# Order of scatters, source gathers and base gathers on POOL in the last edge stage of a four-layer graph network

## The chip, the cores and the metric

The kernel runs on one core of a Trainium2 chip, and its time is the device time of one execution in microseconds (us). A lower number is better. The engines are PE (TensorE), DVE (VectorE), ACT (ScalarE), POOL (GpSimd) and SP (SyncE); each works through its own list of instructions in order, and they wait for one another by semaphores.

## What is computed

The reference is a graph network of four residual layers on 10000 nodes of 512 features and 5000 edges, sorted by the node they go to. Every layer normalises the node rows, and passes messages along the edges. Only the last layer is touched here, by the change as by the prediction:

```
x = inputs @ W_gcn                                  # 512 -> 128
msg = x[src] * edge_attr[:, None]
h = segment_sum(msg, dst, num_segments=N) + b_gcn
return h @ W_fc.T + b_fc                            # 128 -> 512
...
h = jnp.maximum(_layernorm(x, axis=-1), 0.0)
x = x + L3(h, edge_index, edge_weight, W_gcn, b_gcn, W_fc, b_fc)
```

## The kernel before, in words

Stages follow one another: edges and nodes of layer 0, messages, sums and nodes of layer 1, edges and nodes of layer 2, and last `layer3_edges`. The stage before it has already written to `out`, for every node, the row that holds without any edge. `layer3_edges` has to add to those rows of `out` what the edges bring.

The 5000 edges lie in 40 tiles of 128 partitions (`ET`), and four tiles make a group, so that there are 10 groups (`EG`), numbered 0 to 9. The stage's lists of instructions, one for each engine:

- **POOL** issues every transfer of the loop, as indirect DMAs of 128 rows by 512 floats. `rows(g)` (line 2447) gathers the four tiles of source rows of group g from `x3` into `X`, which has room for all 40 tiles. `base(g)` (line 2457) gathers the rows of `out` to which the group will be added into half g % 2 of `Z`; it first waits until the group two earlier has been stored from that half. `finished(g)` (line 2466) waits, tile by tile, for DVE's sum in `Z` and scatters it to `out`. Ahead of the loop stand `rows(0)` to `rows(2)`, `base(0)`, `base(1)` and a gather of 40 further rows into `Zc` (line 2475), and behind it the scatter of `Zc` (line 2485).
- **DVE** has, in `body(g)`, first the statistics of the four tiles of group g + 2 (line 2543), each waiting for its gather; between them the low parts of the transposed rows of group g + 1 (`turned`, line 2562); then the low part of the sums of group g (line 2588), and only then the four sums `Z = z + Z` of group g (`finish`, line 2576), which POOL's scatters wait for.
- **PE** transposes group g + 1 (line 2626), multiplies it by `W_gcn` (`product`, lines 137 to 139 into `m_ps`), and then multiplies the sums of group g by `W_fc` (`out`, lines 137 to 139 into `z_ps`), which `finish` adds. A transpose waits for DVE to have read the buffer that it writes to.
- **ACT** copies between them, and scales the rows of group g + 2.

`body` runs for g = 0 to 7 in full, for 8 without statistics, and for 9 without statistics and transposes. The order of POOL's three pieces in a turn of the loop is written out by hand: `rows(g + 3)`, `finished(g)`, `base(g + 2)`. The order in DVE's `body` is:

```
for j in range(GROUP):
    if norm:
        dve.wait_ge(x_loaded[j], g * 16 + 48)
        stats(g + 2, b, j)
    if turn:
        turned(g + 1, j)
...
finish(g, b, 0)
```

Of the kernel before, what the change touches and what calls it, by code (L numbers as in the profile page):

```python
# [2380 lines left out]
def layer3_edges(nc, core, a, keep, x3, match, out):  # L2381
# [16 lines left out]
    with ExitStack() as st:  # L2398
# [34 lines left out]
        with nc.Block() as block:  # L2433
            @block.sync
            def _(sp):
                sp.dma_start(Wraw[:, :, :], a["L3_gnn_W_gcn"].rearrange("(k p) n -> p k n", p=P)).then_inc(w_loaded, 16)
                sp.dma_start(Wf[:, :], a["WfT"]).then_inc(w_loaded, 16)

            @block.gpsimd
            def _(pool):  # L2440
                def rows(g):

                    for t in range(g * GROUP, g * GROUP + GROUP):
                        if t >= GROUP:
                            pool.wait_ge(x_loaded[t % GROUP], 16 * (t // GROUP))
                            pool.sem_inc(go, 1)
                        pool.indirect_dma_start(X[:, t, :], None, x3[:, :], bass.IndirectOffsetOnAxis(keep["src"][:, t:t + 1], 0),  # L2447
                                                bounds_check=ROWS_N - 1, oob_is_err=False).then_inc(x_loaded[t % GROUP], 16)

                def base(g):  # L2450

                    if g >= 2:
                        pool.wait_ge(stored[g % 2], 64 * (g // 2))
                        pool.sem_inc(go, 1)
                    for j in range(GROUP):
                        t = g * GROUP + j
                        pool.indirect_dma_start(Z[:, g % 2, j, :], None, out[:, :], bass.IndirectOffsetOnAxis(keep["goes"][:, t:t + 1], 0),  # L2457
                                                bounds_check=NODES - 1, oob_is_err=False).then_inc(base_loaded[g % 2], 16)

                def finished(g):  # L2460

                    for j in range(GROUP):
                        t = g * GROUP + j
                        pool.wait_ge(z_out, t + 1 + 2)
                        pool.sem_inc(go, 1)
                        pool.indirect_dma_start(out[:, :], bass.IndirectOffsetOnAxis(keep["goes"][:, t:t + 1], 0), Z[:, g % 2, j, :], None,  # L2466
                                                bounds_check=NODES - 1, oob_is_err=False).then_inc(stored[g % 2], 16)

                for g in range(3):
                    rows(g)  # L2470
                pool.wait_ge(init, 3)
                pool.sem_inc(go, 1)
                base(0)
                base(1)
                pool.indirect_dma_start(Zc[:, :], None, out[:, :], bass.IndirectOffsetOnAxis(keep["head_goes"][:, 0:1], 0),
                                        bounds_check=NODES - 1, oob_is_err=False).then_inc(last_loaded, 16)
                for g in range(EG):
                    if g + 3 < EG:
                        rows(g + 3)
                    finished(g)  # L2480
                    if g + 2 < EG:
                        base(g + 2)
                pool.wait_ge(z_out, ET + 1 + 2)
                pool.sem_inc(go, 1)
                pool.indirect_dma_start(out[:, :], bass.IndirectOffsetOnAxis(keep["head_goes"][:, 0:1], 0), Zc[:, :], None,
                                        bounds_check=NODES - 1, oob_is_err=False).then_inc(last_stored, 16)
                for b in range(2):
                    pool.wait_ge(stored[b], 64 * (EG // 2))
                pool.wait_ge(last_stored, 16)
# [312 lines left out]
```

## Time and profile before

| | |
|---|---|
| median of 3 runs | 2776.52 us |
| lowest, highest | 2774.21, 2776.92 us |
| the profiled execution: its own time | 2777.23 us |
| the profiled execution: its span | 2775.5 us |
| mean granted TensorE clock, share of full | 0.93 |
| busy share of the span: PE, DVE, ACT, POOL | 86%, 57%, 39%, 30% |

A profile shows one execution. The span goes from its first instruction to its last, and its own time is a little longer. Busy shares are means over stages that have different limits. A view of a stretch in time tells which instructions ran there, how long each one took, how long its engine had been idle before it, and what ended that idle time ("<-"). For an indirect DMA on POOL the time shown is that of issuing it; the data land later.

### The profile page before, as it was taken

What the parts mean: (1) busy time and instruction counts of PE and PEld (TensorE: products, weight loads), DVE (VectorE), ACT (ScalarE), POOL (GpSimd) and SP (SyncE); (2) the same over time, 40 slices, a digit from 0 to 9 for tenths busy, and PEclk for the clock granted to TensorE, in tenths of its full rate; (3) what the DMA queues carried; (4) which work ended last, traced back from release to release, by engine and by line L of the source; (5) the groups of instructions that cost most, each with busy time, mean ns of one, the idle gap of its engine ahead of it and who ended that gap; (6) DMA issues with size and microseconds to landing.
All of it is one profiled execution on the core that took longest, in us unless ns stands there. A gap on an engine that the chain in (4) does not pass through costs nothing. (4 is left out here: it accounts for less than half of the span.)

```text
span 2775.5 us, 39392 instructions
## 1 busy us (share of the span) xinstructions
PE 2393.4 (86%) x13443; PEld 2047.9 (74%) x13443; DVE 1568.3 (57%) x3060; ACT 1078.7 (39%) x1858; POOL 825.5 (30%) x684
## 2 busy tenths in 40 slices
PE   7889999999999899999999799955777348999465
PEld 7878888989989789999999688854232237777364
DVE  6733232332323566666666633385999657787554
ACT  2234333333433334333333356633665443333332
POOL 1001010101000211111111144345997345665566
PEclk9999999999999899999999889978888689999788
DMA  6101010101002333323333234324565584766444
GB/s 213 47 9 58 19 57 19 57 19 47 19 15 82 103 112 113 106 105 121 125 133 112 79 110 121 91 79 168 190 218 189 174 278 168 263 250 228 145 153 133
DMA packets 118895, 327.93 MB, mean 118 GB/s; under 512 B 25965, under 2 KB 39405, under 8 KB 100763
## 3 DMA queue, kind: packets, MB, share of 16 engines
q1 hardware_dynamic: 75186, 229.79, 23.0%
q0 software_dynamic: 42336, 97.19, 11.9%
q8 instruction: 39, 0.64, 0.1%
q14 instruction: 38, 0.30, 0.0%
q10 hardware_dynamic: 1296, 0.01, 0.0%
HBM read 245.35 MB, written 128.49 MB: 135 GB/s over the span
## 5 line engine op out<-in xcount | busy, mean ns | idle before, releaser
L137 PE MATMUL b_y_ps<-W23h,b_Rh 128*128 128x320 f32 x800 | 249.2, 311 | 0.0
L138 PE MATMUL b_y_ps<-W23l,b_Rh 128*128 128x320 f32 x800 | 246.0, 308 | 0.0
L139 PE MATMUL b_y_ps<-W23h,b_Rl 128*128 128x320 f32 x800 | 246.0, 308 | 0.0
L1055 POOL DMA_INDIRECT c_G<-T,c_idx x80 | 83.5, 1043 | 452.1 <-DVE c_U L1152 429.8
L137 PE MATMUL b_hid_ps<-b_hTh,W1h 128*128 128x512 f32 x500 | 201.1, 402 | 7.9 <-ACT b_Rh L668 7.9
L137 PE MATMUL c_u_ps<-W1h,c_hTh 128*128 128x320 f32 x640 | 201.2, 314 | 1.0 <-DVE c_U L1152 1.0
L139 PE MATMUL b_hid_ps<-b_hTh,W1l 128*128 128x512 f32 x500 | 199.9, 400 | 0.0
L138 PE MATMUL b_hid_ps<-b_hTl,W1h 128*128 128x512 f32 x500 | 199.9, 400 | 0.0
L138 PE MATMUL c_u_ps<-W1l,c_hTh 128*128 128x320 f32 x640 | 197.7, 309 | 0.0
L139 PE MATMUL c_u_ps<-W1h,c_hTl 128*128 128x320 f32 x640 | 197.7, 309 | 0.0
L766 DVE TENSOR_TENSOR b_Rl<-b_R,b_Rh 128x512 fp32r<-128x512 f32 x100 | 69.2, 692 | 226.9 <-ACT b_Rh L668 226.9
L608 POOL DMA_INDIRECT b_X<-in_x,b_idx x32 | 32.3, 1009 | 490.9 <-PE b_tp_ps L869 482.4
L1966 PE MATMUL n_z_ps<-n_G,n_D 128*128 128x512 f32 x160 | 98.9, 705 | 76.0 <-ACT n_D L1846 32.4
L137 PE MATMUL c_o_ps<-W1h,c_zh 128*128 128x512 f32 x400 | 163.2, 408 | 0.0
L138 PE MATMUL c_o_ps<-W1l,c_zh 128*128 128x512 f32 x400 | 158.0, 395 | 0.0
L139 PE MATMUL c_o_ps<-W1h,c_zl 128*128 128x512 f32 x400 | 157.8, 395 | 0.0
L1092 ACT ACTIVATE c_R<-c_tp_ps,c_b 128x512 f32<-128x512 f32 x100 | 69.0, 690 | 224.7 <-PE c_tp_ps L1235 224.7
L791 DVE TENSOR_TENSOR b_Yl<-b_y_ps,b_Yh 128x320 fp32r<-128x320 f32 x80 | 39.3, 491 | 202.8 <-ACT b_Yh L680 202.8
L138 PEld LDWEIGHTS b_y_ps<-W23l,b_Rh 128*128 128x128 f32 x800 | 150.1, 188 | 0.5
L137 PEld LDWEIGHTS b_y_ps<-W23h,b_Rh 128*128 128x128 f32 x800 | 150.0, 188 | 0.5
L139 PEld LDWEIGHTS b_y_ps<-W23h,b_Rl 128*128 128x128 f32 x800 | 149.9, 187 | 0.0
L667 ACT ACTIVATE b_R<-b_hid_ps,b 128x512 f32<-128x512 f32 x100 | 68.9, 689 | 184.1 <-PE b_hid_ps L139 173.5
(417 smaller groups left out, 6941.4 us busy)
## 6 DMA issues: line engine op xcount, KB each, us to landing
b_X<-in_x SPq DMA_DIRECT2D x21, 1024.0 KB, 5.2
x<-n_O SPq DMA_DIRECT2D x20, 1032.0 KB, 4.9
g_X<-x SPq DMA_DIRECT2D x20, 1032.0 KB, 6.9
x<-c_XB SPq DMA_DIRECT2D x20, 1028.0 KB, 4.5
n_X<-x SPq DMA_DIRECT2D x20, 1028.0 KB, 7.3
x<-g_O SPq DMA_DIRECT2D x20, 1024.0 KB, 3.8
c_XB<-in_x SPq DMA_DIRECT2D x19, 1024.0 KB, 5.4
out<-g_B SPq DMA_DIRECT2D x19, 1024.0 KB, 4.8
```

What stands on the lines that cost most here:

```text
L137: pe.matmul(out, ah, bh, start=first, stop=False)
L138: pe.matmul(out, ah, bl, start=False, stop=False)
L139: return pe.matmul(out, al, bh, start=False, stop=last)
L608: pool.indirect_dma_start(X[:, i // GROUP, i % GROUP, :], None, a["x"][:, :], bass.IndirectOffsetOnAxis(idx[:, i:i + 1], 0), bounds_check= ...
L667: act.activation(R[:, :], hid[:, m % 2, :], ACT.Relu, bias=l0["b1"][:, m:m + 1]).then_inc(relu_ready, 1)
L766: dve.tensor_tensor(Rl[:, m, :], R[:, :], Rh[:, m, :].bitcast(F32), ALU.subtract).then_inc(hid_lo, 1)
L791: dve.tensor_tensor(Yl[:, t % 2, w], y[:, h, 0:HALF], Yh[:, t % 2, w].bitcast(F32), ALU.subtract).then_inc(y_out[h], 1)
L1055: pool.indirect_dma_start(G[:, i // GROUP, i % GROUP, :], None, T0[:, :], bass.IndirectOffsetOnAxis(idx[:, i:i + 1], 0), bounds_check=ROWS ...
L1092: act.activation(R[:, k % 2, :], tp[:, k % 2, :], ACT.Relu, bias=b3[:, c:c + 1]).then_inc(z_hi, 1)
L1966: pe.matmul(z[:, i, :], D[:, g % 2, j, :], G[:, g % RG, j, :], start=True, stop=False)
```

## The change

In each turn of POOL's loop the scatters of group g are issued first, then the source gathers of group g + 3, then the base gathers of group g + 2. Nothing else is changed.

```
                 for g in range(EG):
+                    finished(g)
                     if g + 3 < EG:
                         rows(g + 3)
-                    finished(g)
                     if g + 2 < EG:
                         base(g + 2)
```

POOL's list at the start of the loop, before; `h_X<-x3,src` are the source gathers, `out_0<-h_Z,goes` the scatters, `h_Z<-out_0,goes` the base gathers:

```order
L2447 DMA h_X<-x3,src 128x512 x12
L2457 DMA h_Z<-out_0,goes 128x512 x8
L2475 DMA h_Zc<-out_0,headgoes 40x512
L2447 DMA h_X<-x3,src 128x512 x4
L2466 DMA out_0<-h_Z,goes 10000x512 x4
L2457 DMA h_Z<-out_0,goes 128x512 x4
L2447 DMA h_X<-x3,src 128x512 x4
L2466 DMA out_0<-h_Z,goes 10000x512 x4
```

And in the changed kernel:

```order
L2447 DMA h_X<-x3,src 128x512 x12
L2457 DMA h_Z<-out_0,goes 128x512 x8
L2475 DMA h_Zc<-out_0,headgoes 40x512
L2466 DMA out_0<-h_Z,goes 10000x512 x4
L2447 DMA h_X<-x3,src 128x512 x4
L2457 DMA h_Z<-out_0,goes 128x512 x4
L2466 DMA out_0<-h_Z,goes 10000x512 x4
L2447 DMA h_X<-x3,src 128x512 x4
```

The four source gathers of each turn went from the place before the four scatters to the place between them and the four base gathers.

DVE's list in one turn is the same in both kernels; `h_raw` is written by the statistics, `h_hTl` by `turned`, and `h_Z` by the sums that the scatters wait for:

```order
L2543 BN_STATS h_raw<-h_X 128x6
L2562 TENSOR_TENSOR h_hTl<-h_tp_ps,h_hTh 128x512
L2543 ISA
L2543 BN_STATS h_raw<-h_X 128x6
L2561 REGISTER_ALU
L2562 TENSOR_TENSOR h_hTl<-h_tp_ps,h_hTh 128x512
L2547 ISA
L2550 BN_AGGR h_mv<-h_raw 128x2 x4
L2588 TENSOR_TENSOR h_Sl<-h_s_ps,h_Sh 128x512
L2575 ISA
L2576 TENSOR_TENSOR h_Z<-h_z_ps,h_Z 128x512 x2
```

Nothing moved there: the rows are the first and the last two of the four pairs of statistics and `turned`, and what follows them up to the first sums.

## Rows read from the trace of the kernel before

**Rows 1.** Busy time by stretch: us, PE, PEld, DVE, ACT, POOL, granted clock, DMA share, GB/s.

```profile
2680.00:2698.00 18.00, 11.72 (x60) 10.23 (x60) 9.23 (x21) 6.55 (x11) 12.10 (x13) 0.78 0.48 149
```

**Rows 2.** Timeline of POOL in one turn: start, us, operation [idle before <-releaser].

```profile
2675.26 1.00 POOL L2447 DMA_INDIRECT h_X<-x,src  x1 [0.30 <-issue]
...
2680.47 1.04 POOL L2466 DMA_INDIRECT out<-h_Z,goes  x1 [0.30 <-issue]
...
2684.41 0.98 POOL L2466 DMA_INDIRECT out<-h_Z,goes  x1 [0.30 <-issue]
2687.94 1.04 POOL L2457 DMA_INDIRECT h_Z<-out,goes  x1 [2.54 <-DMA out<-h_Z,goes]
...
2693.21 1.00 POOL L2447 DMA_INDIRECT h_X<-x,src  x1 [0.31 <-issue]
...
2698.42 1.03 POOL L2466 DMA_INDIRECT out<-h_Z,goes  x1 [0.30 <-issue]
```

**Rows 3.** Who waited for whom, 2626 to 2747: us in total, times, longest.

```profile
POOL h_Z L2457 <- DMA out<-h_Z,goes: 17.8, 7, 2.7
```

**Rows 4.** Timeline of DVE and PE in the same turn.

```profile
2678.82 0.69 DVE L2543 BATCH_NORM_STATS2 h_raw<-h_X 128x6 f32 x1 [5.77 <-DMA h_X<-x,src]
...
2683.52 0.63 PE L139 MATMUL h_m_ps<-h_hTh,h_Wl 128*128 128x512 f32 x1
2683.95 0.63 PE L137 MATMUL h_m_ps<-h_hTh,h_Wh 128*128 128x512 f32 x1
...
2687.14 0.40 PE L137 MATMUL h_z_ps<-h_Wfh,h_Sh 128*128 128x512 f32 x1
...
2689.24 1.32 DVE L2576 TENSOR_TENSOR h_Z<-h_z_ps,h_Z 128x512 f32<-128x512 f32 x2
```

**Rows 5.** Timeline of POOL: first source gather of four more turns.

```profile
2639.42 1.00 POOL L2447 DMA_INDIRECT h_X<-x,src  x1 [0.30 <-issue]
...
2657.34 1.00 POOL L2447 DMA_INDIRECT h_X<-x,src  x1 [0.30 <-issue]
...
2711.09 0.99 POOL L2447 DMA_INDIRECT h_X<-x,src  x1 [0.30 <-issue]
...
2729.01 1.00 POOL L2447 DMA_INDIRECT h_X<-x,src  x1 [0.30 <-issue]
```

**Rows 6.** Timeline of DVE: first two sums of a group, in the six turns.

```profile
2652.42 1.29 DVE L2576 TENSOR_TENSOR h_Z<-h_z_ps,h_Z 128x512 f32<-128x512 f32 x2 [2.76 <-PE h_z_ps L139]
...
2669.91 1.29 DVE L2576 TENSOR_TENSOR h_Z<-h_z_ps,h_Z 128x512 f32<-128x512 f32 x2 [2.29 <-PE h_z_ps L139]
...
2687.43 1.29 DVE L2576 TENSOR_TENSOR h_Z<-h_z_ps,h_Z 128x512 f32<-128x512 f32 x2 [2.07 <-PE h_z_ps L139]
...
2705.02 1.29 DVE L2576 TENSOR_TENSOR h_Z<-h_z_ps,h_Z 128x512 f32<-128x512 f32 x2 [1.55 <-PE h_z_ps L139]
...
2722.49 1.29 DVE L2576 TENSOR_TENSOR h_Z<-h_z_ps,h_Z 128x512 f32<-128x512 f32 x2 [1.25 <-PE h_z_ps L139]
...
2741.56 1.29 DVE L2576 TENSOR_TENSOR h_Z<-h_z_ps,h_Z 128x512 f32<-128x512 f32 x2 [2.34 <-PE h_z_ps L139]
```

**Rows 7.** Timeline at the first group: its first two sums, its first scatter.

```profile
2624.86 1.29 DVE L2576 TENSOR_TENSOR h_Z<-h_z_ps,h_Z 128x512 f32<-128x512 f32 x2 [0.87 <-PE h_z_ps L139]
...
2626.50 1.03 POOL L2466 DMA_INDIRECT out<-h_Z,goes  x1 [5.93 <-DVE h_Z L2576]
```

**Rows 8.** By line: one sum; time from a source gather's issue to its landing.

```profile
L2576 DVE TENSOR_TENSOR h_Z<-h_z_ps,h_Z x40: 680/691/694, 2624.9 to 2764.0; 128x512 f32<-128x512 f32 x40
...
DMA to landing us min/median/max: 3.5/3.7/5.2
```

**Rows 9.** Timeline of the end: groups 7 to 9.

```profile
2746.88 1.03 POOL L2466 DMA_INDIRECT out<-h_Z,goes  x1 [0.30 <-issue]
...
2757.39 0.40 PE L139 MATMUL h_z_ps<-h_Wfh,h_Sl 128*128 128x512 f32 x1
...
2761.29 1.29 DVE L2576 TENSOR_TENSOR h_Z<-h_z_ps,h_Z 128x512 f32<-128x512 f32 x2 [4.52 <-DMA h_Z<-out,goes]
```

More of the change, by code:

```diff
@@ L2477, in _ @@
                 for g in range(EG):
+                    finished(g)
                     if g + 3 < EG:
                         rows(g + 3)
-                    finished(g)
                     if g + 2 < EG:
```

## The prediction

> **What bounds the kernel now.** The change touches only the last stage, so I read the busy time by stretch first, then POOL's timeline of one turn, then who waited for whom, and last DVE's and PE's timelines, to see what the instruction behind each wait had itself waited for. In 18 us of the steady loop no compute engine is busy more than 12 us [rows 1]. POOL's list is what sets the pace: from one group's first source gather to the next group's it takes 17.95 us (2675.26 to 2693.21), and almost all of its gaps are the 0.30 us between two issues [rows 2]. One gap is longer: the first base gather waits 2.54 us until the scatters issued before it have landed. It comes in every turn, 17.8 us over 7 of them [rows 3]. Three pieces of four issues and this wait make the turn. One piece takes 5.2 us: source gathers 2675.26 to 2680.47, 5.21; scatters 3.94 to the start of the fourth, and 0.98 and 0.30 for it and its gap, 5.22; base gathers 2687.94 to 2693.21, 5.27, the first of them 0.05 longer after the wait. Of a turn without that wait 15.7 us would be left.
>
> The same rows tell that DVE waits for POOL: its first statistics instruction sat idle 5.77 us until the first source gather had landed, 3.56 us after its issue [rows 2, 4]. The sums that the scatters need come later in DVE's list than these statistics. Now the scatters don't feel that: the first sums of that turn begin at 2687.43, and the scatter that wants them is issued at 2698.42, 10.3 us after the first is done at 2688.12 (0.69 us for one) [rows 2, 6, 8].
>
> **The change part by part.** No instruction is added or taken away; 28 source gathers (seven turns of four) move behind 28 scatters.
>
> The wait for the scatters' landing: the source gathers now stand between the scatters and the base gathers. They take 5.21 us, and the wait was 2.54 us, so the base gathers find the scatters landed. Gain: up to 2.5 us in each of seven turns. Turn 7 has no source gathers, and its wait stays.
>
> The new order closes a loop. Source gathers of group g + 3 used to be issued before the scatters of group g, which need nothing from them. They are now issued after them, and the next thing but the base gathers is the scatters of group g + 1. These need the sums of group g + 1, which in DVE's list stand behind the statistics of group g + 3. Each turn is then, from scatter to scatter:
>
> - first sum done to first scatter issued: POOL is idle and waits, as it did for the first group. The sum ends at 2624.86 + 0.69 = 2625.55, and the scatter starts at 2626.50 [rows 7, 8]: 0.95 us.
> - four scatters, until the first source gather: 5.22 us.
> - first source gather issued to the first sum begun. Six turns show it while DVE waits for the gather, as it will: 13.00, 12.57, 12.17, 11.81, 11.40 and 12.55 us (each start in rows 6 less the gather's in [rows 2, 5]), on average 12.25.
> - the first sum: 0.69 us [rows 8].
>
> Together 19.11 us. The fourth sum is done 2.4 us after the first (2689.24 + 1.32 against 2688.12 [rows 4]) and the fourth scatter starts 3.9 us after the first, so only the first sum counts. POOL's own work of 15.7 us fits into this, and POOL will stand idle for about 3.4 us ahead of each first scatter; queued behind that wait are the source gathers on which DVE waits in turn. DVE, PE and ACT get nothing new to do, and their work is inside the 12.25 us.
>
> Sum: from the first scatter of group 0 to that of group 7 it took 2746.88 - 2626.50 = 120.38 us [rows 7, 9]. The first group's scatter stays where it is, because its sums wait for nothing that moves; POOL waited 5.93 us for them already [rows 7]. Seven turns of 19.11 make 133.77, which is 13.39 us more. A part of that comes from the last of the seven, which held no source gathers before, and now does.
>
> The end: from the first scatter of group 7 the base gathers of group 9 follow as before, and 14.41 us after that scatter the sums of group 9 begin (2761.29), having waited 4.52 us for those gathers [rows 9]. This wait was cover for PE, and it shrinks: PE's product for that sum was ready at 2757.79, 15.54 us after the first sum of group 7 (2741.56 + 0.69) [rows 6, 9]. With the scatter now 0.95 us behind that sum, the gathers are in at 15.36. So PE is late by 0.2 us, and the tail grows by that. In all +13.6 us against the profiled execution's 2777.23 us: 2790.8. The median of the runs is 0.7 us below that execution, so I forecast **2790.1 us**, 0.49% slower.
>
> What no row shows is the landing of a gather issued straight behind four scatters; in the trace source gathers follow base gathers. The nearest rows give 3.5 at least and 5.2 us at most, with a median of 3.7 [rows 8]. I take the 3.56 us that is in the 12.25, because the queue carried the same bytes at the same pace before; with 5.2 us in each turn the sum would grow by 11.5 us, and a gain from it of more than 0.4 us in all is excluded by the minimum.
>
> The Trainium skill (DMA: Bandwidth & Descriptors, Anatomy of one DMA — SWDGE (gpsimd) path) gives 2.0 us plus the bytes at 436 GB/s for one transfer, an estimate of 2.6 us for these 256 KB; by that the turn would be 18.15 us and the time 2783.4. The trace has 3.56 us for this very transfer, so I keep 2790.1.
>
> **The rivals.** (a) Faster. The loop doesn't close, and POOL's issuing stays the bound: the turn shrinks to 15.7 us, seven take 109.9, and the time is 10.5 us lower, 2766.0. That holds if the first sum is done within 9.5 us of the first source gather's issue (two pieces of POOL's work, 10.4, less 0.95). For it speaks that the wait of 2.5 us is plainly on POOL's path [rows 2, 3]; against it, that the shortest of six turns needed 11.40 + 0.69 = 12.09. The Trainium skill (Perfetto Trace Analysis, Optimization Strategy) says to find the gaps on the engine that limits a stretch and make what ends them start or finish sooner, and by that rule this rival is the outcome. The gap is there as the rule wants it, but closing it puts another wait on the same engine. 5%.
>
> (b) No change. The new wait costs what the old one did: 17.9 us a turn from the first group on, seven times, make 125.3 us, 4.9 us more and 2781.4. For that, 11.0 us from gather to sum are needed, less than any of the six showed. 4%.
>
> (c) Slower still. PE's gap between groups grows with the turn. Its granted clock is 0.78 over this stretch [rows 1]: after the gap its matmuls start 0.43 us apart (2683.52, 2683.95), which is the lower level of 1.2 GHz. Later in the same turn it is back on the upper one: the 13 starts after 2683.52 take 3.62 us to 2687.14, and at 0.43 us each they would take 5.6 [rows 4]. If the clock stayed low through product and output, the 12.17 us of this turn would thus be 14.2. That is a turn of 21.0 us, and the time is 2803.5. Against it: none of the six turns came near 14.2. Late landings (5.2 us) end near the same time, 2801.6. 8% together.
>
> **How the numbers follow.** The forecast, a loop through DVE, has the remaining 83%. Its own bounds: all turns like the shortest (11.40) give 7.4 us more through the loop, 2784.1; all like the longest (13.00) give 18.6 more, 2795.3. The unpriced landing can add to that, so the range goes from 2784 to 2797; it leaves out (a), and most of (c). Measurement can tell about 0.2%, 5.5 us, from no change: faster 0.05, same 0.04, slower 0.91.
>
> **What would show it.** Right: first scatters about 19.1 us apart from 2626.5 on; the line of waits from base gathers to scatters down to one of 2.5 us, in turn 7; in its place a wait of scatters for DVE's sums, some 3.4 us in each turn; DVE's statistics still waiting for the source gathers, longer than 5.8 us. Wrong: scatters 15.7 us apart with no idle time before them would mean (a); a turn of 21 us with PE at 0.43 us a matmul up to the sums, or landings above 3.7 us, would mean (c).

## The result, and the profile after

The changed kernel takes 2786.99 us (median of 6 runs, 2785.44 to 2788.76), the kernel before 2775.36 us (6 runs, 2772.15 to 2776.92). The ratio is 1.0046 with a 95% interval of 1.0035 to 1.0058: slower by 11.6 us, where 13.6 were forecast, and inside the range of 2784 to 2797.

The profiled execution of the changed kernel took 2787.22 us. First, POOL's timeline: the first scatter of each of the groups 0 to 7.

```profile
2623.75 1.04 POOL L2466 DMA_INDIRECT out<-h_Z,goes  x1 [11.11 <-DVE h_Z L2576]
...
2642.36 1.02 POOL L2466 DMA_INDIRECT out<-h_Z,goes  x1 [3.17 <-DVE h_Z L2576]
...
2661.82 1.02 POOL L2466 DMA_INDIRECT out<-h_Z,goes  x1 [4.07 <-DVE h_Z L2576]
...
2680.15 1.02 POOL L2466 DMA_INDIRECT out<-h_Z,goes  x1 [2.94 <-DVE h_Z L2576]
...
2699.43 1.02 POOL L2466 DMA_INDIRECT out<-h_Z,goes  x1 [3.88 <-DVE h_Z L2576]
...
2717.74 1.02 POOL L2466 DMA_INDIRECT out<-h_Z,goes  x1 [2.94 <-DVE h_Z L2576]
...
2737.32 1.02 POOL L2466 DMA_INDIRECT out<-h_Z,goes  x1 [4.20 <-DVE h_Z L2576]
...
2757.04 1.02 POOL L2466 DMA_INDIRECT out<-h_Z,goes  x1 [4.32 <-DVE h_Z L2576]
```

The starts lie 18.61, 19.46, 18.33, 19.28, 18.31, 19.58 and 19.72 us apart, 133.29 us in all, where the kernel before took 120.38 [rows 7, 9]. In groups 1 to 7 each first scatter now stands behind an idle time of 2.9 to 4.3 us that a sum of DVE ends. Before, these scatters had only the 0.30 us between issues [rows 2]. Group 0 is apart: POOL waits 11.11 us instead of 5.93 [rows 7] there, because four source gathers no longer fill the first 5.2 us of that wait.

The rest of the turn from 2661.82 to 2680.15, on POOL and then on DVE:

```profile
2665.74 0.99 POOL L2466 DMA_INDIRECT out<-h_Z,goes  x1 [0.30 <-issue]
2667.03 1.05 POOL L2447 DMA_INDIRECT h_X<-x,src  x1 [0.30 <-issue]
2668.39 1.01 POOL L2447 DMA_INDIRECT h_X<-x,src  x1 [0.31 <-DMA out<-h_Z,goes]
...
2672.31 0.99 POOL L2457 DMA_INDIRECT h_Z<-out,goes  x1 [0.31 <-issue]
```

```profile
2670.64 0.69 DVE L2543 BATCH_NORM_STATS2 h_raw<-h_X 128x6 f32 x1 [7.27 <-DMA h_X<-x,src]
...
2678.55 1.29 DVE L2576 TENSOR_TENSOR h_Z<-h_z_ps,h_Z 128x512 f32<-128x512 f32 x2 [1.31 <-PE h_z_ps L139]
```

The base gathers follow the source gathers after 0.31 us; the 2.54 us of [rows 2] are gone from this place. DVE's first statistics sat idle 7.27 us (5.77 in [rows 4]), until the gather issued at 2667.03 had landed, 3.61 us later. The sums begin 11.52 us after that gather. Over the seven turns this is 11.77, 12.65, 11.52, 12.47, 11.51, 12.46 and 12.91 us, on average 12.18.

Who waited for whom, from 2626 to 2760 (total, times, longest), and then, from the lines of the gathers, what base gathers of the whole stage waited for, and how long source gathers took to land:

```profile
DVE h_raw L2543 <- DMA h_X<-x,src: 50.6, 15, 7.6
...
POOL out L2466 <- DVE h_Z L2576: 26.4, 10, 4.3
```

```profile
DMA out<-h_Z,goes: 2.5, 1
```

```profile
DMA to landing us min/median/max: 3.4/3.6/5.4
```

The wait of [rows 3], 17.8 us over 7 times, has shrunk to a single one of 2.5 us, in turn 7. In its place stand 26.4 us in which POOL waits for sums. Source gathers land about as fast behind scatters as they did behind base gathers (3.5/3.7/5.2 in [rows 8]).

The last turns, on POOL and on DVE:

```profile
2764.40 1.05 POOL L2457 DMA_INDIRECT h_Z<-out,goes  x1 [2.45 <-DMA out<-h_Z,goes]
...
2778.73 0.99 POOL L2466 DMA_INDIRECT out<-h_Z,goes  x1 [0.30 <-issue]
2780.02 0.96 POOL L2485 DMA_INDIRECT out<-h_Zc,headgoes  x1 [0.30 <-issue]
```

```profile
2755.44 1.29 DVE L2576 TENSOR_TENSOR h_Z<-h_z_ps,h_Z 128x512 f32<-128x512 f32 x2 [2.71 <-PE h_z_ps L139]
...
2772.07 1.29 DVE L2576 TENSOR_TENSOR h_Z<-h_z_ps,h_Z 128x512 f32<-128x512 f32 x2 [1.48 <-DMA h_Z<-out,goes]
```

From the first scatter of group 7 to the end of the span (2785.4) it is 28.36 us, and it was 28.62 before (2775.5 less 2746.88). The sums of group 9 begin 15.03 us after that scatter instead of 14.41, and the end doesn't feel it: from the base gathers on POOL issues one DMA after the other with 0.30 us between them, to the last. From the first scatter of group 7 to that of group 9 it is 17.84 us in both kernels. The difference of 0.26 us lies behind that, and no run here explains it.

The spans of the two profiled executions differ by 9.9 us (2785.4 and 2775.5): 12.91 through the loop, -0.26 in the tail, and -2.75 up to the first scatter (2623.75 and 2626.50), because this one reached the stage earlier. Its first source gather was issued at 2583.6 and not at 2586.3, though nothing ahead of the stage differs. From that gather to the first scatter both took 40.2 us.

### The profile page after: what moved, and what is told of

It reads as the page before. It is cut to its first block and busy times, and to the rows that moved or that the text cites. A ratio compares the mean times of both kernels' runs of the same rounds, so it can differ in the third digit from the quotient of the medians.

```text
span 2785.4 us, 39392 instructions
## 1 busy us (share of the span) xinstructions
PE 2394.3 (86%) x13443; PEld 2052.5 (74%) x13443; DVE 1568.4 (56%) x3060; ACT 1077.8 (39%) x1858; POOL 825.2 (30%) x684
## 3 DMA queue, kind: packets, MB, share of 16 engines
q0 software_dynamic: 42336, 97.19, 11.8%
```

## The experiments

The kernel before and the changed one differ in two things at once. Read round the loop, the list before is scatters of g, base gathers of g + 2, source gathers of g + 4. The changed one has the source gathers in front of the base gathers, and they are those of g + 3. The first two experiments do one of these each. Their edits, and that of the last experiment, are shown against the kernel before; those of the other two against the changed kernel.

**The swap alone.**

```
+                rows(3)
                 for g in range(EG):
-                    if g + 3 < EG:
-                        rows(g + 3)
                     finished(g)
+                    if g + 4 < EG:
+                        rows(g + 4)
                     if g + 2 < EG:
                         base(g + 2)
```

> Source gathers between scatters and base gathers, as in the changed kernel, but one group earlier: rows(3) ahead of the loop, then finished(g), rows(g+4), base(g+2). Theory (the loss comes from the lost lead of the source gathers, which closes a loop through DVE's statistics): the loop stays open, the gathers cover the scatters' landing, and POOL's issuing is the bound: first scatters 15.7 us apart in the first six turns and 12.7 in the seventh, 106.9 us from group 0 to group 7 against 120.4 before, so about 13 us below the kernel before, 2762. Rival (source gathers straight behind scatters are what costs, by late landing or by the queue): turns as in the changed kernel, 18.3 to 19.7 us, 2787, or at best no gain over the kernel before.

Measured: 2763.11 us, ratio to the kernel before 0.9947 (0.9934 to 0.9961). POOL's timeline of one turn, and the first base gather of turn 6, in which no source gathers are left:

```profile
2657.22 1.03 POOL L2466 DMA_INDIRECT out<-h_Z,goes  x1 [0.30 <-issue]
...
2661.15 0.99 POOL L2466 DMA_INDIRECT out<-h_Z,goes  x1 [0.30 <-issue]
2662.45 1.04 POOL L2447 DMA_INDIRECT h_X<-x,src  x1 [0.30 <-issue]
...
2667.72 1.00 POOL L2457 DMA_INDIRECT h_Z<-out,goes  x1 [0.30 <-issue]
...
2672.93 1.04 POOL L2466 DMA_INDIRECT out<-h_Z,goes  x1 [0.30 <-issue]
```

```profile
2727.41 1.05 POOL L2457 DMA_INDIRECT h_Z<-out,goes  x1 [2.50 <-DMA out<-h_Z,goes]
```

The turn is 15.71 us, and POOL has no gap in it but the 0.30 us between issues. Where no source gathers cover it, the wait for the scatters is back with its 2.50 us. So the place behind the scatters costs POOL's turn nothing here, and the swap by itself is worth 2.2 us a turn.

**The lead alone.**

```
                 for g in range(EG):
-                    if g + 3 < EG:
-                        rows(g + 3)
                     finished(g)
                     if g + 2 < EG:
                         base(g + 2)
+                    if g + 3 < EG:
+                        rows(g + 3)
```

> The order of pieces of the kernel before (scatters, base gathers, source gathers, read round the loop), but the source gathers one group later: finished(g), base(g+2), rows(g+3). Theory: the loop closes, now with the landing wait and the base gathers inside it as well: 0.95 + 5.22 + 2.5 + 5.27 + 12.25 + 0.69 = 26.9 us a turn, seven turns 188 us against 120.4 before, about 68 us above the kernel before, 2843. Rival (the place straight behind the scatters is what costs): turns of 17.9 us as before, 2776.

Measured: 2839.58 us, ratio 1.0224 (1.0209 to 1.0240). One turn on POOL:

```profile
2676.30 1.02 POOL L2466 DMA_INDIRECT out<-h_Z,goes  x1 [8.89 <-DVE h_Z L2576]
...
2683.76 1.05 POOL L2457 DMA_INDIRECT h_Z<-out,goes  x1 [2.54 <-DMA out<-h_Z,goes]
...
2689.04 1.00 POOL L2447 DMA_INDIRECT h_X<-x,src  x1 [0.30 <-issue]
...
2703.10 1.02 POOL L2466 DMA_INDIRECT out<-h_Z,goes  x1 [9.16 <-DVE h_Z L2576]
```

The seven turns take 185.7 us (2623.96 to 2809.69), 26.5 each where 26.9 were expected. Against the changed kernel the source gathers are issued later by the wait and four base gathers, 7.8 us, and the turn is longer by 7.5 (26.5 less 19.0). A source gather that is late by a microsecond now makes the turn about a microsecond longer. A lost group of lead thus costs 8.6 us a turn in the old order (17.9 to 26.5) and 3.3 us in the new one (15.7 to 19.0); the swap gives back a part of it, and the lead accounts for the loss.

**The loop opened at its other end.** The changed kernel's list on POOL stays, and DVE's order is changed: the first two sums of group g now stand ahead of the statistics of group g + 2.

```
                     for j in range(GROUP):
-                        if norm:
-                            dve.wait_ge(x_loaded[j], g * 16 + 48)
-                            stats(g + 2, b, j)
                         if turn:
                             turned(g + 1, j)
...
                     finish(g, b, 0)
                     finish(g, b, 1)
+                    if norm:
+                        for j in range(GROUP):
+                            dve.wait_ge(x_loaded[j], g * 16 + 48)
+                            stats(g + 2, b, j)
+                        mean(g + 2, b)
+                        scale(g + 2, b)
                     if turn:
                         weigh(g + 1)
```

On ACT `messages(g + 1)` goes ahead of `root` and `norm_rows`; the two lists were only changed together. As a control the same was done with POOL's list of the kernel before.

> POOL's list of the changed kernel, unchanged, with the same lead of three groups; DVE's list in a turn reordered: turned, low part of the sums, the first two sums of group g, and only then the statistics of group g+2, weigh and the last two sums; ACT copies the messages ahead of scaling the next rows. Theory (the loop closes because the sums stand behind the statistics in DVE's list): the first two scatters no longer wait for the gather, the last two wait until about 9.9 us after the first gather's issue instead of 14, so POOL's issuing is nearly the bound: turns of 15.7 to 17 us instead of 18.3 to 19.7, 2764 to 2773. Rival (the lead itself, or the place behind the scatters, sets the turn whatever DVE's order): turns of 18.3 to 19.7, 2787.

> The same DVE and ACT order with POOL's list of the kernel before: control. Theory: POOL's issuing with the landing wait is the bound there, so the turns stay at 17.9 us and the time at 2776, within 3 us. Rival (the new order of DVE and ACT is shorter in itself, wherever the gathers stand): turns below 17.5 us and a time below 2773.

Measured: with the changed kernel's list 2778.31 us, ratio to the kernel before 1.0013 (1.0004 to 1.0022); with the old list 2779.17 us, ratio 1.0013 (1.0004 to 1.0023). Who waited for whom in the first of them, 2626 to 2747, and its POOL around one turn:

```profile
DVE h_hTl L2560 <- ACT h_hTh L2506: 36.1, 27, 3.3
...
PE h_tp_ps L2623 <- ACT h_H L88: 9.4, 7, 1.5
...
POOL out L2466 <- DVE h_Z L2574: 13.3, 7, 3.1
```

```profile
2678.06 1.03 POOL L2466 DMA_INDIRECT out<-h_Z,goes  x1 [0.30 <-issue]
...
2682.01 0.98 POOL L2466 DMA_INDIRECT out<-h_Z,goes  x1 [1.62 <-DVE h_Z L2574]
...
2695.09 1.02 POOL L2466 DMA_INDIRECT out<-h_Z,goes  x1 [0.30 <-issue]
```

Waits of DVE for source gathers, 50.6 us in the changed kernel, don't occur in this list at all. In groups 1 to 7 the first scatter waits for nothing, and the turn settles at 17.0 us (after 18.6 and 17.5 for the first two). With the lead and POOL's order unchanged, the new order on DVE and ACT takes 8.7 us off the changed kernel (2786.99 to 2778.31), so DVE's list is part of the loop, as the theory has it. Taken as pairs, POOL's new order costs 11.6 us with the old order on DVE and ACT, and nothing that can be measured with the new one (2778.31 against the control's 2779.17).

The time expected (2764 to 2773) was missed by 5 us. I had left out that the scaling of the next rows on ACT, which used to lie beside PE's products, now stands between the statistics and PE's transposes. One round of that chain, from the statistics of one group to those of the next, on DVE, ACT, PE and DVE:

```profile
2675.97 2.46 DVE L2541 BATCH_NORM_STATS2 h_raw<-h_X 128x6 f32 x4
...
2680.03 2.93 ACT L88 ACTIVATE h_H<-h_X,h_shift,h_rstd 128x512 f32 x4 [0.63 <-DVE h_shift L2555]
...
2683.09 1.11 PE L2623 MATMUL h_tp_ps<-ident,h_H 128*128 128x128 f32 x4 [1.33 <-ACT h_H L88]
...
2691.86 1.29 DVE L2574 TENSOR_TENSOR h_Z<-h_z_ps,h_Z 128x512 f32<-128x512 f32 x2 [1.65 <-PE h_z_ps L139]
...
2693.07 2.46 DVE L2541 BATCH_NORM_STATS2 h_raw<-h_X 128x6 f32 x4
```

It takes 17.1 us, and in the chain that ended last from 2676 to 2693 no instruction of POOL and no transfer occurs: this round is the new bound. The last turns became longer too, 15.4 and 6.4 us instead of 12.6 and 5.2, together 4.0 us; the cause of that is open. The control has turns of 17.9 us from the second on, as expected, so the new order is not shorter in itself there; its first turn is 21.9 instead of 18.1 us, which fits the 4 us by which its time lies above the kernel before, where I had allowed 3.

**The clock.** The changed kernel with matmuls in PE's gap, for which PE's loop is also written out; the writing out was not run by itself:

```
                             turn(g + 1, 1 - b, j)
+                        if fill and j == 1:
+                            for _ in range(28):
+                                pe.matmul(m[:, :], Wfh[:, 0:P], Wfh[:, :], start=True, stop=True)
```

> The changed kernel, with 28 further matmuls of 128x512 on PE in each of the groups 1 to 7, where PE waits for DVE (their result is overwritten), so that PE is not idle there; PE's loop is written out. It is to tell how much of a turn is the clock coming back after PE's gap. Theory: with the clock on its upper level the first sum is ready 11.2 us or less after the first source gather instead of 12.1 on average, turns even out at 17.6 to 18.3 us instead of 18.3 to 19.7, and the time falls by 4 to 9 us against the changed kernel, to 2778 to 2783; it does not come below the kernel before by more than 2 us, since the loop is still closed. Rival (the clock's return is beside the path, and landings make the difference between turns): turns keep 18.3 to 19.7 us, 2787.

Measured: 2781.08 us, ratio to the kernel before 1.0018 (1.0009 to 1.0027), 5.9 us below the changed kernel. Busy time over two turns, of the changed kernel and then of this one (us, PE, PEld, DVE, ACT, POOL, granted clock, DMA share, GB/s):

```profile
2642.40:2680.20 37.80, 23.17 (x121) 20.06 (x120) 18.59 (x40) 12.91 (x23) 24.08 (x25) 0.77 0.45 143
```

```profile
2641.50:2677.50 36.00, 33.43 (x178) 26.80 (x177) 19.04 (x40) 13.07 (x23) 24.04 (x24) 1.00 0.48 151
```

And one turn of this kernel, from its first source gather to the next group's first scatter:

```profile
2664.72 1.04 POOL L2447 DMA_INDIRECT h_X<-x,src  x1 [0.31 <-issue]
...
2677.50 1.02 POOL L2466 DMA_INDIRECT out<-h_Z,goes  x1 [2.61 <-DVE h_Z L2576]
```

```profile
2675.90 1.29 DVE L2576 TENSOR_TENSOR h_Z<-h_z_ps,h_Z 128x512 f32<-128x512 f32 x2 [0.88 <-PE h_z_ps L139]
```

With PE kept busy the granted clock is 1.00 over both turns, the upper level, and the sums begin 11.18 us after the gather, 11.0 to 11.2 in each of the seven turns. All seven turns last 17.9 to 18.2 us. The two views below are of the changed kernel again, from the first source gather to the first sum in a short turn and in the long one after it:

```profile
2667.03:2678.55 11.52, 6.57 (x29) 5.86 (x30) 6.24 (x15) 3.14 (x6) 8.04 (x8) 0.70 0.60 176
2685.36:2697.83 12.47, 7.65 (x29) 6.58 (x30) 6.25 (x16) 4.01 (x8) 8.06 (x8) 0.59 0.57 166
```

The granted clock is 0.70 or 0.71 in the three stretches of 11.5 to 11.8 us, and 0.59 or 0.60 in the four of 12.5 to 12.9. In the short turn PE's matmuls of 128x512 start 0.23 us apart, the upper level, from the third of `product` on, at 2675.27; in the long one they start 0.41 to 0.43 us apart, the lower level, up to the eighth, at 2695.67. So the unevenness of the changed kernel, 18.3 to 19.7, comes from where in PE's work the clock returns. The return costs about 1 us a turn on average (19.0 against 18.0), and it is on the path because the loop runs through PE. By their times, the reordered lists and the held clock can't be told apart (1.0013 and 1.0018, with intervals that overlap); what differs is the waits, and the turns, 17.0 against 18.0 us.

**One more group of lead.**

```
+                rows(3)
+                rows(4)
                 for g in range(EG):
-                    if g + 3 < EG:
-                        rows(g + 3)
                     finished(g)
+                    if g + 5 < EG:
+                        rows(g + 5)
                     if g + 2 < EG:
                         base(g + 2)
```

> As the swap alone, with one more group of lead: rows(3) and rows(4) ahead of the loop, where POOL waits 5.9 us for the first sums, then finished(g), rows(g+5), base(g+2). Theory (POOL's issuing is the bound once the loop is open): five turns of 15.7 us and two of 12.7, 103.9 us from group 0 to group 7, 16.5 us less than before, 2760. Rival (PE, DVE and ACT become the bound at less than 15.7 us of work, or the first scatter comes later by the added 5.2 us): no better than the swap alone, 2762 or more.

Measured: 2760.18 us, ratio to the kernel before 0.9943 (0.9929 to 0.9956). Its first scatter, the first base gather of turn 5, and DVE's longest wait:

```profile
2626.04 1.03 POOL L2466 DMA_INDIRECT out<-h_Z,goes  x1 [0.74 <-DVE h_Z L2578]
...
2712.03 1.04 POOL L2457 DMA_INDIRECT h_Z<-out,goes  x1 [2.52 <-DMA out<-h_Z,goes]
```

```profile
DVE h_Z L2578 <- DMA h_Z<-out,goes: 30.5, 7, 6.2
```

The wait before the first scatter has shrunk from 5.93 us [rows 7] to 0.74, five turns take 15.7 us, and turn 5 with its wait of 2.52 us takes 12.7. DVE now waits for base gathers, that is, for POOL. The time is 15 us below the kernel before and 27 below the changed one. The swap alone lies within its interval, so the times don't tell the two versions apart; in the traces the way from the first scatter of group 0 to that of group 7 is 103.95 us here (103.9 expected) and 106.87 there.

## Why the prediction was right

The mechanism and the size came out as forecast; one small term, the tail, did not.

- **The wait that goes.** As forecast: the base gathers find the scatters landed, and the wait remains in turn 7 only.
- **The loop.** Forecast as 19.11 us a turn; measured 19.04 on average. Of its terms, 0.95 was 0.91 (2757.04 less 2755.44 + 0.69, the first sum of group 7), 5.22 was 5.21 (2661.82 to 2667.03), and 12.25 was 12.18. The swap alone, the lead alone and the reordered lists on DVE and ACT show that both ends are needed: the late gather, and the sums behind the statistics. That the averages agree to 0.1 us is in part luck: the six rows behind the 12.25 spread from 11.40 to 13.00, the seven turns after from 11.51 to 12.91, and both hold the clock's return, about 1 us, which the forecast took over with the rows and priced only in rival (c).
- **The unpriced landing.** The 3.56 us that I took were right; it is 3.61 in the turn shown, and the median is 3.6. The Trainium skill's fit (DMA: Bandwidth & Descriptors, Anatomy of one DMA — SWDGE (gpsimd) path) would have given an estimate of 2.6 us and 2783.4 in all, below every run; the measurement decides.
- **The first group.** Forecast to stay; 40.2 us after the first source gather in both.
- **The tail.** This step failed, by half a microsecond: I had the tail grow by 0.2 us because PE's product would be late. It didn't grow. The sums of group 9 still waited for their base gathers, 1.48 us, not for PE, and they are not on the path: POOL's issuing is, with the same 17.84 us from group 7 to group 9. That the whole tail came out 0.26 us shorter lies behind that stretch, and its cause is open.
- **The size.** 13.6 us forecast; 12.65 by the profiles (loop and tail), 11.6 by the medians, whose interval reaches from 9.7 to 16.1 us (0.35% to 0.58% of 2775.4).
- **Rival (a)**, POOL's issuing as the bound at 15.7 us, is what happens as soon as the lead is kept. There the Trainium skill's rule on gaps that I set beside it (Perfetto Trace Analysis, Optimization Strategy) holds: the gap of 2.5 us is closed, and the turn falls from 17.9 to 15.7 us. The changed kernel closes the same gap and loses, because the same edit puts another wait on the same engine. **Rival (b)** would need sums 11.0 us after the gather. Even with the clock held they took 11.1 and the time stayed 0.18% above the kernel before, so (b) nearly describes that experiment, not the change. **Rival (c)** didn't occur: no turn came to 21 us.

## What to carry to other kernels

When a piece of a hand-written list is moved past a wait, count in groups how far ahead of its use it is issued afterwards: here one line's move cost a whole group of lead, and with that a transfer's latency and a chain through three engines came to stand inside every turn. The gain and the loss of such an edit can be taken apart, and here the gain was had by moving the piece, adding one group to its index and issuing that group ahead of the loop. Then price the chain from the issue to the wait it feeds by rows of the kernel before in which the engine behind it already sits idle for that transfer; here these gave the turn to 0.1 us, closer than their own spread of 1.6 us lets one expect.

## What the runs showed that I had not expected

- The same code ahead of the stage reached it at times that differ by 5.7 us between profiled executions: the first source gather was issued at 2580.6 us in the control, at 2583.6 in the changed kernel and at 2586.3 in the kernel before. For changes of this size the distances inside the stage are the better measure, and single spans mislead.
- In the changed kernel longer and shorter turns alternate (18.61, 19.46, 18.33, 19.28, 18.31, 19.58), and with PE kept busy they are all alike, 17.9 to 18.2 us.
